# Splitting a late quantization into halves, GpSimd work into pieces, and reordering the prologue of a cross-attention and FP4 feed-forward kernel

## The reference

```python
def fp4_quant_dequant(x):                       # blocks of 16 along the last dim
    scale = jnp.maximum(jnp.max(jnp.abs(xb), axis=-1, keepdims=True) / 6.0, 1e-12)
    xn = xb / scale
    idx = jnp.searchsorted(_MID, jnp.abs(xn))
    q = _GRID[idx] * jnp.sign(xn) * scale
...
attn = softmax(einsum('bhqd,bhkd->bhqk', q, k) * scale)
x = x + (einsum('bhqk,bhkd->bhqd', attn, v)) @ Wo.T + bo      # q from layernorm(x), k and v from ctx
h = silu(fp4_linear(ln(x), w_gate)) * fp4_linear(ln(x), w_up)
x = x + fp4_linear(h, w_down)
```

## Time and profile before

| | us |
|---|---|
| median of 3 runs (1790.6 to 1791.48) | 1791.18 |
| the profiled execution, its time | 1790.86 |
| its span, first to last instruction | 1789.1 |
| TensorE busy | 1658.9 (93%) |
| VectorE busy | 1432.7 (80%) |
| ScalarE busy | 1133.2 (63%) |
| GpSimd busy | 526.3 (29%) |

### The profile page before, as it was taken

How to read it: one execution, slowest core, us unless ns; L and a number is a source line. 1 busy time by engine, 2 the same in 40 slices (tenths; PEclk the granted TensorE clock), 3 DMA queues, 4 the chain that set the end, 5 groups by cost and what they waited for, 6 DMA issues and landing times.

```text
span 1789.1 us, 26605 instructions
## 1 busy us (share of the span) xinstructions
PE 1658.9 (93%) x9408; PEld 655.9 (37%) x9408; DVE 1432.7 (80%) x2032; ACT 1133.2 (63%) x2293; POOL 526.3 (29%) x409
## 2 busy tenths in 40 slices
PE   4798889999999999999999999999999999989968
PEld 2332224333433334333443334333443333313325
DVE  6777888878778887879888787788878797788538
ACT  2367567766667667676667666676676766666631
POOL 4316340442107220253204421072202531012203
PEclk8899899999999999999999999999999999999989
DMA  5644432142324313352331423244132422200000
GB/s 147 147 71 110 97 83 44 47 111 57 61 43 108 86 34 55 60 128 48 64 56 51 109 55 61 43 109 89 32 60 54 91 46 53 54 7 10 13 21 12
DMA packets 106224, 117.50 MB, mean 66 GB/s; under 512 B 22884, under 2 KB 87404, under 8 KB 106092
## 3 DMA queue, kind: packets, MB, share of 16 engines
q1 hardware_dynamic: 101408, 111.54, 29.5%
q10 hardware_dynamic: 4684, 4.27, 1.0%
HBM read 76.78 MB, written 30.16 MB: 60 GB/s over the span
## 4 chain that ended last, share of the span: by engine, by line
PE 77%; DVE 12%; ACT 5%; issue 3%; DMA 1%; ACTq 0%; POOL 0%; SPq 0%; DVEq 0%; POOLq 0%
PE pvb L780 20%; PE st L751 20%; PE mx L765 10%; PE misc L687 7%; DVE cmx L1012 5%; PE misc L645 5%; PE misc L652 5%; ACT prob L937 4%; PE misc L699 2%; PE misc L707 2%; PE misc L666 2%; PE misc L695 1%; PE misc L631 1%; PE misc L728 1%; DVE ht L1041 1%
## 5 line engine op out<-in xcount | busy, mean ns | idle before, releaser
L937 ACT ACTIVATE prob<-st 128x512 f32<-128x512 f32 x1630 | 886.5, 598 | 425.2 <-PE st L751 422.6
L1012 DVE TENSOR_REDUCE cmx<-mx 128x2 f32<-128x1024 f32 x768 | 906.1, 1220 | 194.7 <-PE mx L765 191.6
L751 PE MATMUL st<-qstack,kstack 112*128 112x512 bf16 x1630 | 514.1, 387 | 36.2 <-ACT prob L937 23.5
L780 PE MATMUL pvb<-prob,vv 128*32 128x512 f32 (+1 forms) x3328 | 446.7, 609 | 0.6 <-ACT prob L937 0.6
L751 PEld LDWEIGHTS st<-qstack,kstack 112*128 112x128 bf16 x1630 | 130.2, 99 | 527.6 <-issue 255.0
L765 PE MATMUL mx<-kstack,qstack 48*128 48x512 bf16 (+1 forms) x2048 | 254.7, 339 | 26.9 <-DMA qstack<-scr_q 15.8
L1315 POOL TENSOR_TENSOR ht<-ht,rh 128x704 f32<-128x704 f32 x29 | 40.3, 1388 | 420.5 <-DVE rh L988 420.5
L687 PE MATMUL misc<-wguT,rowsT 128*128 128x352 f32 x456 | 153.7, 458 | 0.0
L1279 POOL TENSOR_TENSOR cin<-cin 128x400 f32<-128x400 f32 (+1 forms) x60 | 55.3, 922 | 278.7 <-ACT cin L872 278.7
L765 PEld LDWEIGHTS mx<-kstack,qstack 48*128 48x128 bf16 x2048 | 57.9, 94 | 198.2 <-issue 154.5
L780 PEld LDWEIGHTS pvb<-prob,vv 128*32 128x32 f32 (+1 forms) x3328 | 66.0, 109 | 138.8 <-issue 124.0
(11 more groups left out here) (196 smaller groups left out, 1564.4 us busy)
## 6 DMA issues: line engine op xcount, KB each, us to landing
kstack<-scr_k SPq DMA_DIRECT2D x384, 100.1 KB, 4.4
scr_k<-cin SPq DMA_DIRECT2D x48, 300.0 KB, 3.4
qstack<-scr_q SPq DMA_DIRECT2D x372, 32.0 KB, 1.9
cin<-ctx_in SPq DMA_DIRECT2D x8, 1280.0 KB, 6.6
scr_q<-qp SPq DMA_DIRECT2D x15, 384.0 KB, 5.4
scr_k<-cin SPq DMA_DIRECT2D x16, 300.8 KB, 5.3
xn<-x SPq DMA_DIRECT2D x8, 512.0 KB, 3.9
att<-pvs SPq DMA_DIRECT2D x128, 32.0 KB, 1.9
```

The costliest lines, as they stand in the source:

```text
L751: mm(score_bank(it, n, pair, h)[0:KROWS[kt], :], kstack[:, hd, KOFF[kt]:KOFF[kt] + KROWS[kt]], qstack[:, hd, :], start=True, stop=True).th ...
L780: last = mm(pvb[2 * D * h:2 * D * (h + 1), :], vv[0:w, kt, (HG * g + h) // 2, D * (h % 2):D * (h % 2 + 2)], prob[0:w, n % 2, h, :], start= ...
L937: activate(prob[0:KROWS[kt], n % 2, 2 * pair + h, :], score_bank(it, n, pair, h)[0:KROWS[kt], :], ACT.Exp, scale=SCALE).then_inc(exp_done[ ...
L1012: v.tensor_reduce(cmx[:, g % 2, h0:h0 + 2, at:at + 1], products, op=ALU.max, axis=AX.X).then_inc(max_free, 1)
```

## The change

**Steps.** `o` 1 and the first `xnT` change places. The row quantization of the late batch is done for two tiles of 128 rows (512 columns) at a time; each half's rounding constant lies in its own part of `ht`, not in `mt`, so it no longer waits for the query projection. `nm` 3 and `values` 3 move a step or two later. In the tail VectorE does one layer norm for all four tiles and then the halves. **GpSimd.** Instructions of 704 or 1024 columns become pieces of 352 or 256; the bias add becomes four; the fills go by head. **Prologue.** The context comes in five transfers, not three; the transposed input and the first query projection stand behind four context pairs, ahead of the rest of the context and of the keys; the first query parts are written out by SyncE, not by ScalarE; the second fill also waits for the key split. **Weights.** Every second weight piece has its rounding constant in `rowsT`.

```diff
+PIECES = [0, 2, 6, 10, NKT - 1]
 SLOTS:
-    6: ([("o", 1, "late")], []),
-    7: ([("xnT", 0, "early")], []),
+    6: ([("xnT", 0, "early")], []),
+    7: ([("o", 1, "late")], []),
 PRE_SLOTS:
-    5: ([("ctx2", j, "early") for j in range(7)], []),
-    8: ([("xnT", j, "early") for j in range(2)], []),
+    5: ([("ctx2", j, "early") for j in range(3)] + [("xnT", j, "early") for j in range(2)] + [("ctx2", 3, "early")], []),
+    9: ([("q", 0, "early")], []),
+    10: ([("ctx2", j, "early") for j in range(4, 7)], []),
     11: ([("k", j, "early") for j in range(4)], []),
-    14: ([("q", 0, "early")], []),
 DVE_EXTRA:
...
-    7: [("late", "mean", 0)], 8: [("late", "root", 0)], 9: [("late", "apply", 0)], 10: [("att", "nm", 1)], 11: [("late", "apply", 1)], 12: [("late", "xmax", 0)],
-    13: [("late", "xscale", 0)], 14: [("late", "xmul", 0)], 15: [("late", "xpower", 0)], 17: [("late", "xlast", 0)],
+    7: [("late", "stats", 1), ("late", "mean", 0)], 8: [("late", "root", 0)], 9: [("late", "apply", 0)], 10: [("att", "nm", 1)],
+    11: [("late", "xscale", 0)], 12: [("late", "xpower", 0)], 13: [("late", "apply", 1)], 14: [("late", "xscale", 1)], 15: [("late", "xpower", 1)],
+    16: [("late", "xlast", 0)], 17: [("late", "xlast", 1)],
 POOL_WORK:
-    0: [("late", "bias", 0)], 10: [("early", "k", 0)], 11: [("early", "k", 1)], 12: [("early", "q", 0)], 13: [("early", "k", 2)],
-    14: [("early", "k", 3)], 15: [("early", "k", 4)], 16: [("late", "xround", 0)], 17: [("early", "k", 5), ("early", "q", 1)], 18: [("early", "k", 6)], 19: [("early", "k", 7)],
+    0: [("late", "bias", 0)], 10: [("early", "k", 0)], 11: [("early", "k", 1)], 12: [("early", "q", 0)], 13: [("late", "xround", 0), ("early", "k", 2)],
+    14: [("early", "k", 3)], 15: [("early", "k", 4)], 16: [("late", "xround", 1), ("early", "q", 1)], 17: [("early", "k", 5)], 18: [("early", "k", 6)], 19: [("early", "k", 7)],
 TAIL_EXTRA:
-    3: [("late", "half", 0)], 4: [("late", "half", 1)],
+    3: [("late", "stats", 0)],
+    4: [("late", "stats", 1), ("late", "mean", 0), ("late", "root", 0)] + [("late", what, k) for k in range(2) for what in ("apply", "xscale", "xpower", "xlast")],
 prologue, SyncE:
                 sp.wait_ge(c_link, 4)
+                queries_out(it, 0)
                 keys_out(it, 0, range(4))
 GpSimd:
-                g_.memset(kstack[32:64, heads, :].bitcast(F32), 1.0 + 2.0 ** -23 * 0x3F80).then_inc(c_link, 1)
+                for hd in range(heads.start, heads.stop):
+                    last = g_.memset(kstack[32:64, hd, :].bitcast(F32), 1.0 + 2.0 ** -23 * 0x3F80)
+            def short(out, in0, in1, op):
+                n = out.shape[1] // 256
+                w = out.shape[1] // n
+                for j in range(n):
+                    cols = slice(j * w, (j + 1) * w)
+                    last = g_.tensor_tensor(out[:, cols], in0[:, cols], in1[:, cols], op)
+                return last
...
-                        pool.wait_ge(xm_ready, c(1, 1))
-                        g_.tensor_tensor(xa[:, :], xa[:, :], m, ALU.add).then_inc(xr_step, 1)
+                        pool.wait_ge(xm_ready, c(2, k + 1))
+                        short(y, y, m, ALU.add).then_inc(xr_step, 1)
...
                     if it.kind == "pre" and n == 15:
+                        pool.wait_ge(k_split[0], 4)
                         pool.wait_ge(q_split, 1)
```

More of the change, by code:

```diff
@@ L681, in shared @@
                             pe.wait_ge(free["wT"], 2 * WPIECES)
-                        if kind == "gate" and it.kind == "tail" and half == 0:
+                        if kind == "gate" and half == 0:
                             pe.wait_ge(free["xqT"], c(2, t // 2 + 1))
-                        elif kind == "gate" and j == 0:
-                            pe.wait_ge(free["xqT"], c(2, 2))
                         for h in range(NC2):
@@ L723, in context_tile @@
                     _, j, part = job
-                    if j in (0, 2, NKT - 1) or j == 8 and it.kind == "first":
-                        pe.wait_ge(s_ctx[0 if j == 0 else 2 if j == NKT - 1 else 1], it.count(part, 16, 16))
+                    if j in PIECES or j == 8 and it.kind == "first":
+                        pe.wait_ge(s_ctx[max(p for p in range(len(PIECES)) if PIECES[p] <= j)], it.count(part, 16, 16))
                     w, o = KROWS[j], job_bank(it, job)
@@ L880, in take @@
                     elif kind == "xqT":
[L881 to L884 removed]
+                        last = copy(rowsT[:, :, 256 * j:256 * (j + 1)], src.rearrange("p (c n) -> p c n", c=NC2))
                     elif kind == "gate":
@@ L1262, in fill @@
             def fill(heads, done):
-                g_.memset(kstack[32:64, heads, :].bitcast(F32), 1.0 + 2.0 ** -23 * 0x3F80).then_inc(c_link, 1)
-                g_.memset(qstack[32:64, heads, :].bitcast(F32), 0.0).then_inc(c_link, 1)
+                for hd in range(heads.start, heads.stop):
+                    last = g_.memset(kstack[32:64, hd, :].bitcast(F32), 1.0 + 2.0 ** -23 * 0x3F80)
+                last.then_inc(c_link, 1)
+                for hd in range(heads.start, heads.stop, 2):
+                    last = g_.memset(qstack[32:64, hd:hd + 2, :].bitcast(F32), 0.0)
+                last.then_inc(c_link, 1)
                 pool.wait_ge(c_link, done)
@@ L1274, in bias_columns, with short_scaled @@
                 last.then_inc(bvl_ready, 1)
+            def short(out, in0, in1, op):
[5 more added lines that the diff above has]
+                return last
+            def short_scaled(y, sc):
+                n = y.shape[1] // 256
+                w = y.shape[1] // n // NB
+                for j in range(n):
+                    part = blocks(y)[:, j * w:(j + 1) * w, :]
+                    last = g_.tensor_tensor(part, part, over(sc[:, j * w:(j + 1) * w]), ALU.mult)
+                return last
             def body(it):
```

152 lines of the change are left out of this document (61 added, 91 removed).

## The result

The changed kernel takes 1811.34 us (median of 4 runs, 1809.44 to 1814.66) against 1790.93 us before. The ratio is 1.0116, 95% interval 1.0098 to 1.0133. I had predicted 1777 us and a range that ended at 1790: wrong in sign. The profiled execution took 1810.14 us, its span is 1808.3 us.

The account below looks back on a forecast made before the run. TensorE sets the pace, busy 202.35 of 208.00 us a loop iteration. 21.4 + 7.7 - 23.4 - 3 + 5 + 5 + 1 = 13.7 us gained, from 1790.9 to 1777 us; range 1756 to 1790.

Parts of the forecast that it names:

- Stall B stays: Loop step 19: TensorE's 0.98 us wait for exponentials becomes 1.5 us; 3 us lost in six iterations (bounds 0, 9).
- Halves, the first new stall: Before step 15's scores: ScalarE waits for key job 2's split behind half of `xround`; 2.4 us idle, 23.4 us lost.
- Swap: Step 6: `o` 1's 1.98 us wait for `att` and the slow clock behind it go; 21.4 us gained.
- `nm` 3 and `values` 3: Step 37: `hqT` 4's 1.22 us wait falls to about 0.1 us; 7.7 us gained over seven times.
- Pieces: GpSimd's cut instructions cost nothing extra; in "first" VectorE waits less for them, 5 us gained (bounds 1 and 8).
- Prologue: Before the loops: first products start near 37.3 us; 5 us gained (bounds 2.5 and 6).
- Tail: End of the kernel: shorter waits for GpSimd leave 1 us gained (bounds 3 gained, 1.5 lost).
- the new wait is bigger: Rival: GpSimd, shut out by VectorE, ends `xround` and split 3 us later; 24 us more, 1801 us; chance 0.08.
- The first rival: Key job 2's split isn't late for ScalarE; 23.4 and 3 us come back, 1751 us; chance 0.15.
- only the loops count: Rival: prologue, "first" and tail give nothing; 11 us less gained, 1788 us; chance 0.15.

Follow-up runs that it names:

- e11_k5_first: Changed kernel with only GpSimd's splits of query 1 and key job 5 put ahead of the second half of `xround` (`xlast` 1 a step later); 1789.61 us.
- e1_order: Changed kernel, GpSimd's key job 2 split ahead of `xround`'s first half, query 1 and key job 5 splits ahead of its second (`xlast` 1 later); 1762.79 us.
- e6_k2_first: Changed kernel with only GpSimd's split of key job 2 put ahead of the first half of `xround`; 1789.88 us.
- e12_query_last: e6_k2_first with GpSimd's split of query 1 also put back behind key job 5's; 1755.97 us.
- e2_whole: Changed kernel with GpSimd's quantization instructions whole again instead of in pieces; 1809.39 us.
- e10_order_whole: e1_order with GpSimd's quantization instructions whole instead of in pieces; 1764.01 us.
- e9_bits_later: e1_order with, on VectorE, the second half's two exponent instructions a step later (16) and `xlast` 0 at step 17; 1755.61 us.
- e4_swap_nm: Kernel before with only `o` 1 and the first `xnT` exchanged, `nm` 3 at step 36 and `values` 3 at step 38; 1762.17 us.

## Why the prediction was wrong

**The step that failed is "Stall B stays".** It read: "ScalarE stands 1.8 us rather than 1.3 behind TensorE's key job 7. I take 1.5 us of TensorE for 0.98: 6 x 0.5 = 3 us lost (bounds 0 and 9)." Measured, this stall is 3.03 us of idle time and a clock of 0.70 over 5.7 us behind it, which costs another 1.7 us. That is 3.75 us more than the 0.98 before, 22.5 us in six iterations where 3 were forecast. Taking the stall away gives 21.7 us (e11_k5_first), 27.1 (e1_order against e6_k2_first) or 33.9 (e12_query_last against e6_k2_first). Two errors add up in it.

The first is the size of the wait. ScalarE took key job 7 3.38 us behind TensorE's (790.67 less 787.29), where it had been 1.33: 2.05 us later, and 0.5 were forecast. The prediction names the query's split ahead of key job 5 but not the terms of its addition, so it doesn't show which of them was too small. The rows show what moved, counted from ScalarE's take of query 1. The second half of `xround` starts 5.42 us on (780.45 less 775.03), where the whole one had started 4.59 on (772.99 less 768.40): 0.8 us later. It takes 3.41 us for the whole one's 4.8 (two instructions of 2.36 and a gap): 1.4 less. The query's split adds 3.5, and key job 5's own split is 0.4 shorter. In all 2.5 us later, against a TensorE that comes 0.5 later itself. The query's split is the largest of these, and e12_query_last shows that without it the stall is gone.

The second error is of another kind: with 3 us of idle time for 1 the stall got a slow clock of its own, which I had given to the first stall only.

**Halves, the first new stall.** Place, cause and price were right: 2.4 us idle and 23.4 in all were predicted, 3.29 idle were measured, and 21.5 to 26.8 us in all. The 0.9 us between are half VectorE (its `xpower` ended 9.4 us behind the take of query 0, where I had 8.9) and half `xround`: 2.90 us against 2.4, of which 0.28 are the pieces and the rest is that two instructions of 512 columns take 2.62 us and not 2.36 (e2_whole). The slow clock came behind four of the six only, and cost 1.7 us where it came (0.70 over 5.6 us). A scale computation of VectorE took 1.15 us there instead of 0.2, with the query's split on GpSimd. Its timeline, and the last instruction of `xpower` 0:

```profile
758.22 1.15 DVE L988 SCALAR_TENSOR_TENSOR sx<-ax,tiny 128x32 f32<-128x32 f32 x1
...
763.47 0.43 DVE L1130 TENSOR_SCALAR ht<-ht 128x512 f32<-128x512 f32 x1
```

**Swap.** Right: 24.25 us for 21.4. **`nm` 3 and `values` 3.** Right in the loops (1.07 us an iteration for 1.1), 4.3 for 7.7 in all; one of its seven times isn't there.

**Pieces.** "So nothing" was wrong: each instruction that cutting adds costs 0.17 to 0.20 us, and GpSimd is busy 561.5 us with pieces and 527.4 whole (e2_whole). Two copies of 128 columns were too little to read a fixed part from. The estimate of 60 ns that I had worked out from the Trainium skill (GPSIMD Engine Reference, 3.1) had the sign right and a third of the size; the table there names two software steps of dispatch for GpSimd, without a figure for them. Off the path that costs nothing that can be measured (e10_order_whole); in front of a key split it is 0.28 and 0.79 us. What pieces give in "first" was right in kind, `nmr` down from 2.46 to 0.83 us, and at about 2 us smaller than the 5 of the sum.

**Prologue.** 5 us predicted, 2.2 measured. The first products come 3.8 us earlier (5.1 expected). What I missed is what follows: from there to the first scores it is 38.66 us where it was 36.92, and three of the projections that stand between now wait for ScalarE, 1.08, 0.59 and 1.12 us; that these waits are the reason is read from the rows and wasn't tested. **Tail.** 1 us predicted, 0 measured.

**The sum.** Gains: 24.2 + 4.3 + 2.2 + 2.2 + 0 = 32.9 us where I had 40.1. The changed kernel is 20.4 us slower, so halves and their order cost 53.3 us where I had 26.4. Of the 34 us between forecast and result, 27 are these two stalls, and nearly all of that is stall B: the first stall alone is 21.5 to 26.8 us against the 23.4 forecast. The other 7 us are the smaller gains.

**The rivals.** The second, "the new wait is bigger", had chance 0.08; it is what happened: slower by more than the 2.3 us an iteration from which it decides. But it put 3 us of growth on the first stall and at most one on B, and measured are 0.9 and 1.5 us beyond my forecast. Its mechanism, GpSimd shut out between pieces, isn't what made the first stall: four pieces took 2.90 us, 0.72 each, which is their plain price. In the second half four pieces took 3.41 us, so at most 0.5 us there can be such a shutting out. The first rival did not happen. The third, "only the loops count", was more right than my forecast on its point: of the 11 us for prologue, "first" and tail 4.4 came.

With GpSimd's order put right the idea works: e9_bits_later and e12_query_last take 1755.6 and 1756.0 us, 2.0% less than before (ratio intervals 0.9787 to 0.9814). Of these 35 us, 28.5 are the two moves of e4_swap_nm. The other 7 are halves, pieces, prologue and tail together; no run has the two moves and the halves alone. Why the stretch "first" differs by up to 2 us between kernels with the same work there stays open; the clock falls behind some of its stalls in one kernel and not in another, but no run tells why.

## What to carry to other kernels

When work is split so that its first half can start early, write out the queue of the engine that does it as a time table from one fixed event, with everything that is moved past everything else. Here a half of `xround` (2.9 us, and the wait for its input) was moved ahead of one split, and a split of 3.5 us ahead of another: each made ScalarE late, at some 4 us in each of six iterations. The order put right gave 55 us (e12_query_last), without a change in any instruction.

An engine that is busy 31% of the time can still set the pace where two engines wait for it in a row; look for the end of its instruction just ahead of an idle time whose bracket says "issue".

Where a stall grows from one microsecond to three, cost the slow clock behind it too: here it added half of the stall (1.7 us to 3.03) to four fifths of it (2.85 to 3.48). And look at every occurrence, not at one: behind equal stalls of 1.9 to 3.3 us the clock fell in some iterations and not in others.
